# A graph network of four layers on one core: second layer's output and gate by nodes, scores straight from h, one accumulation for coordinates, taps with high passes first, and a new timetable of steps

## The chip, the cores and the metric

One NeuronCore of one Trainium2 chip. The metric is device time in microseconds (us) for one execution, which handles 16 graphs of 512 nodes with 128 features. TensorE is called PE, VectorE DVE, ScalarE ACT, GpSimd POOL, and SyncE, which only issues transfers here, SP.

## The reference

Each layer l does `h = relu(layernorm(x)); x = x + L_l(h, adj)`, for graphs of 512 nodes. Cut to what matters:

```python
# layer 0: attention with 8 heads over the adjacency, sigmoid at the end
# layer 1
h' = h @ W_w.T + W_b
e = (h' @ A) @ h'.T;  e = e + e.T
att = softmax(where(adj > 0, e, NEG), axis=1) * adj
hp = relu(att @ h')
c = sigmoid(h . gate_w[:128] + hp . gate_w[128:] + gate_b)     # one number per node
out = c * h + (1 - c) * hp
# layer 2: 5 times a message over adj and a GRU cell
# layer 3
xc = relu(bn2(conv17(relu(bn1(conv1(h))))) + h)
s = h @ w_se.T + b_se                                          # 3 coordinates
dist = |s_n|^2 + |s_m|^2 - 2 s_n . s_m;  nmp = (exp(-dist) * adj) @ relu(h @ w_msg.T + b_msg)
out = gru([xc, nmp], h)
```

## The kernel before, in words

**Slots.** Graph g uses the buffers and the four banks of accumulator memory (`banks`, B) of slot g % 2, so at most two graphs are in flight. A graph goes through `values`, `keys`, `heads`, `layer1`, `layer2`, `layer3` and `taps` on PE and through functions of the same kind on the other engines.

**Order.** Each engine has a set of generators per graph. The code between two `yield`s is one step. `in_order` (L145) merges all steps of all graphs into one fixed queue per engine, by the due times in `TURN` (L86) plus `g * GAP` (L83). The due times set the order of the queue and nothing else: every step still waits on semaphores. A step that waits holds back all that is queued behind it on its engine. There are 180 PE steps for a graph.

**Precision.** A weight or an activation is split into a high and a low part (fp32r), and a product takes three matmuls, `mm3` (L440): `high` (L445) issues high x high and low x high, `low` (L450) issues the third. Other products are plain f32. In the trace an f32 matmul shows as two MATMUL records, a transpose or an fp32r matmul as one.

**Layer 0, heads.** Each head has four tiles: DVE adds the mask and takes a minimum (L1087), ACT does a Prelu and an Exp (L802, L808), DVE a reciprocal (L1099), POOL multiplies (L395), PE transposes (L551), DVE and ACT copy (L1109, L820), PE multiplies (L557).

**Layer 1** (PE L574 to L634, ACT L822 to L851, DVE L1111 to L1197, POOL L398 to L414). h is transposed to features by nodes; h' (`h1`, L593) comes from it, then t1 = (A + A^T) h' (L598), then four score tiles (L583 to L587), each masked with a maximum on DVE (L1120), negated (L1126) and exponentiated on ACT (L838). After the fourth, DVE takes reciprocals (L1169) and scales all four tiles of h' (L1173), DVE and POOL multiply by the adjacency (L1132, L411), and PE sums hp over four tiles as features by nodes, 128x512 each (L623). The gate is two f32 matmuls with gate_w broadcast to all 128 columns (L617, L628), a 128x512 tanh (L845), two DVE operations (L1183, L1186), four transposes back (`transpose_out`, L632), an add to the residual X (L1043), then statistics, rstd on POOL (L365), normalising (L1017) and transposes for layer 2 (L634, L484). POOL also rebuilds h as one f32 tile (`whole`, L367), for L617, L1179 and, in layer 3, for L704, L713 and L1281.

**Layer 3.** Coordinates come from h by an f32 matmul (L704), their squares (L903) by two more with a matrix of -1, and twice the coordinates by another (L713 to L716), into two banks, each split by ACT and DVE (L910, L914, L1275). The convolution of 17 taps is 17 times mm3 (`taps`, L755). After it come `c2_scaled` (L1281), two Relus on ACT (L926, L927), and the matmuls of the gates (L740 to L750).

## Time and profile before

| | |
|---|---|
| median of 3 runs | 2485.11 us (2477.29 to 2489.0) |
| the profiled execution's own time | 2485.19 us |
| its span, first to last instruction | 2483.4 us |
| busy: PE, DVE, ACT, POOL | 88%, 66%, 62%, 32% |
| granted TensorE clock, mean | 0.945 of full |
| transfers (DMA) | 65.44 MB, mean 26 GB/s |
| chain that ended last | PE 60%, DVE 20%, ACT 9%, issue 8%, POOL 3% |

A busy PE is not PE at its peak: matmuls are pipelined and their records overlap, so what one costs is read from start to start. The granted clock has two levels here, full (2.4 GHz) and half (1.2 GHz). The chain that ended last is followed back from the last instruction, at each step to what released it.

### The profile page before, as it was taken

How to read it: one execution, taken by the hardware profiler on the slowest of the kernel's cores; microseconds unless marked ns; L12 is line 12 of the kernel's file. 1: busy time of each engine (PE TensorE's matmuls, PEld its weight loads, DVE VectorE, ACT ScalarE, POOL GpSimd, SP SyncE). 2: the span in 40 equal slices, each digit the busy share in tenths (PEclk: the TensorE clock that was granted, in tenths of full speed). 3: DMA queues.
4: the chain of work that ended last, by engine and by line, in shares of the span. 5: the costliest groups of instructions: out<-in, count | busy, mean ns of one | idle time of the engine just before them, and what ended most of it. 6: DMA issues, size and time to landing. Idle time of an engine off the chain costs nothing.

```text
span 2483.4 us, 35526 instructions
## 1 busy us (share of the span) xinstructions
PE 2191.5 (88%) x12414; PEld 1800.1 (72%) x12414; DVE 1635.4 (66%) x4499; ACT 1551.5 (62%) x2980; POOL 782.5 (32%) x865
## 2 busy tenths in 40 slices
PE   4779999899999989999899989989998998999866
PEld 3658777686877868777686867768687776868644
DVE  3557676675767767576775758677576767767542
ACT  1738476583856748485684848668484765848432
POOL 0323324233332423334232333424233342423311
PEclk7979999999999999999999999999999999999988
DMA  3010101010010100000010010101001010100100
GB/s 109 18 39 1 34 26 35 26 31 14 17 35 26 35 26 18 22 22 35 26 35 26 1 35 27 35 26 35 26 1 35 26 35 26 35 9 1 35 5 5
DMA packets 46788, 65.44 MB, mean 26 GB/s; under 512 B 3728, under 2 KB 21392, under 8 KB 46352
## 3 DMA queue, kind: packets, MB, share of 16 engines
q1 hardware_dynamic: 46608, 63.16, 7.8%
q8 instruction: 98, 1.61, 0.3%
q14 instruction: 82, 0.67, 0.1%
HBM read 58.96 MB, written 4.19 MB: 25 GB/s over the span
## 4 chain that ended last, share of the span: by engine, by line
PE 60%; DVE 20%; ACT 9%; issue 8%; POOL 3%; DMA 0%; DVEq 0%; SPq 0%; ACTq 0%
PE banks L557 12%; PE banks L447 8%; PE banks L448 8%; PE banks L451 8%; PE banks L551 6%; PE banks L660 3%; PE banks L664 2%; PE banks L736 2%; DVE F L1217 2%; POOL rstd L365 2%; PE banks L623 2%; ACT F L856 2%; DVE F L1224 2%; PE banks L647 2%; DVE F L1204 1%
## 5 line engine op out<-in xcount | busy, mean ns | idle before, releaser
L557 PE MATMUL banks<-F,PT 128*128 128x128 f32 x4096 | 568.4, 283 | 37.6 <-DVE PT L1109 34.5
L557 PEld LDWEIGHTS banks<-F,PT 128*128 128x128 f32 x4096 | 527.8, 198 | 68.1 <-DVE PT L1109 47.0
L856 ACT ACTIVATE F<-banks,dcols 128x512 f32<-128x512 f32 x288 | 196.2, 681 | 162.7 <-PE banks L451 161.2
L395 POOL TENSOR_SCALAR U<-U,rden 128x512 f32<-128x512 f32 x192 | 151.4, 791 | 330.7 <-DVE rden L1099 330.7
L1109 DVE COPY PT<-banks 128x512 f32<-128x512 f32 x256 | 175.3, 685 | 62.2 <-PE banks L551 61.2
L395 POOL TENSOR_SCALAR tiles<-tiles,rden 128x512 f32<-128x512 f32 x192 | 132.8, 694 | 183.4 <-DVE rden L1099 183.3
L820 ACT ACTIVATE PT<-banks 128x512 f32<-128x512 f32 x256 | 150.9, 589 | 53.5 <-PE banks L551 51.9
L551 PE MATMUL banks<-ident,U 128*128 128x128 f32 x768 | 126.3, 295 | 65.0 <-POOL U L395 65.0
L1099 DVE RECIPROCAL rden<-den 128x1 f32<-128x1 f32 x512 | 80.2, 158 | 131.6 <-ACT tiles L808 64.5
L447 PE MATMUL banks<-R,WH 128*128 128x512 f32 x352 | 157.1, 446 | 3.7 <-DVE R L1289 2.9
L1204 DVE SCALAR_TENSOR_TENSOR F<-F 128x512 f32<-128x512 f32 x96 | 71.0, 739 | 133.0 <-ACT F L856 133.0
L551 PEld LDWEIGHTS banks<-ident,U 128*128 128x128 f32 x768 | 100.6, 154 | 75.3 <-POOL U L395 69.1
L802 ACT ACTIVATE tiles<-tiles,QN 128x513 f32<-128x513 f32 x192 | 137.2, 715 | 20.5 <-DVE tiles L1087 20.5
L395 POOL TENSOR_SCALAR adjT<-adjT,rden 128x512 f32<-128x512 f32 x128 | 88.9, 694 | 192.4 <-DVE rden L1099 192.4
L447 PE MATMUL banks<-HS,WH 128*128 128x512 f32 x336 | 147.7, 440 | 1.4 <-ACT HS L783 1.4
L808 ACT ACTIVATE tiles<-tiles 128x512 f32<-128x512 f32 x192 | 138.7, 722 | 13.4
L451 PE MATMUL banks<-R,WH 128*128 128x512 f32 x352 | 145.6, 414 | 0.0
L808 ACT ACTIVATE U<-U 128x512 f32<-128x512 f32 x192 | 138.2, 720 | 9.6
L421 POOL TENSOR_TENSOR HS<-HT,HS 128x512 fp32r<-128x512 f32 x64 | 83.0, 1297 | 193.9 <-ACT HS L885 193.9
L802 ACT ACTIVATE U<-U,QN 128x513 f32<-128x513 f32 x192 | 137.4, 716 | 9.1 <-DVE U L1087 9.0
L448 PE MATMUL banks<-R,WLO 128*128 128x512 f32 x352 | 141.6, 402 | 0.0
L448 PE MATMUL banks<-HS,WLO 128*128 128x512 f32 x336 | 140.2, 417 | 0.0
(217 smaller groups left out, 5574.2 us busy)
## 6 DMA issues: line engine op xcount, KB each, us to landing
adjN<-in_adj_dram SPq DMA_DIRECT2D x32, 1024.0 KB, 5.2
adjT<-in_adjt_dram SPq DMA_DIRECT2D x16, 1024.0 KB, 5.2
xin<-in_x_dram SPq DMA_DIRECT2D x18, 256.0 KB, 2.8
out_dram<-X SPq DMA_DIRECT2D x16, 256.0 KB, 2.3
F<-in_c2w_dram SPq DMA_DIRECT2D x1, 1088.0 KB, 7.7
F<-in_wraw_dram SPq DMA_DIRECT2D x1, 1024.0 KB, 9.4
PT<-in_fcw_dram SPq DMA_DIRECT2D x1, 512.0 KB, 3.8
PT<-in_fpw_dram SPq DMA_DIRECT2D x1, 512.0 KB, 4.6
```

What stands on the lines that cost most here:

```text
L395: pool.tensor_scalar(SC[s][h % RING][:, t, 0:NODES], SC[s][h % RING][:, t, 0:NODES], rden[s][:, t:t + 1], 1.0, ALU.mult, ALU.mult).then_in ...
L447: pe.matmul(dst, w[0], xs[0], start=start, stop=False)
L448: pe.matmul(dst, w[1], xs[0], start=False, stop=False)
L451: return pe.matmul(dst, w[0], xs[1], start=False, stop=stop)
L551: last = pe.transpose(pt_bank(s, j)[:, part(t)], SC[s][h % RING][:, t, part(j)], ident[:, :])
L557: last = pe.matmul(B[s][:, 3, part(j)], PT[s][:, k, part(j)], G[s][:, k, h * DIM:(h + 1) * DIM], start=(h == 0 and j == 0 and k == 0), sto ...
L802: act.activation(SC[s][h % RING][:, t, :], SC[s][h % RING][:, t, :], ACT.Prelu, bias=QN[s][:, t, h:h + 1], scale=0.01, alpha=100.0).then_i ...
L808: act.activation(SC[s][h % RING][:, t, 0:NODES], SC[s][h % RING][:, t, 0:NODES], ACT.Exp, bias=SC[s][h % RING][:, t, NODES:NODES + 1], sca ...
L820: act.activation(PT[s][:, j, :], pt_bank(s, j), ACT.Copy).then_inc(S["pt_act"], 1)
L856: act.activation(F[s][:, tile, :], B[s][:, bank, :], func, bias=dcol(bias), scale=0.5)\
L1109: dve.tensor_copy(PT[s][:, j, :], pt_bank(s, j)).then_inc(S["pt_dve"], 1)
L1204: dve.scalar_tensor_tensor(F[s][:, 3, :], F[s][:, 0, :], 1.0, F[s][:, 2, :], ALU.add, ALU.mult)\
```

## The change

What it does, by parts:

1. **Scores straight from h.** W_w^T (A + A^T) is multiplied out once in the setup (`WA`), so that t1 (negated) comes from h in the same PE step as h', and not from h'. The signs are turned: DVE adds +9e15 and takes a minimum, ACT uses it as a bias with scale -1, and the negation (L1126) is gone.
2. **Output by nodes.** Reciprocals and scaling go tile by tile. hp is summed with the attention as the stationary operand: 4 x 4 f32 matmuls of 128 columns in place of 4 of 512.
3. **Gate by nodes.** The two gate matmuls, the 128x512 tanh and the four transposes back go. In their place: 2 x 4 dot products with accumulation on DVE (128x128), a 128x4 tanh on ACT, two 128x512 adds on POOL, and four 128x128 operations on DVE that write X.
4. **Coordinates in one accumulation.** mm3 with `se` and one f32 matmul of 4 rows in place of four f32 matmuls. POOL's `whole` is no longer waited for there; in layer 1 it is gone.
5. **Taps.** 17 steps of `high` (two matmuls) that wait only for the high part of the first convolution, then 17 steps of `low`. POOL adds the batch norm's shift to h ahead of time (`x_shift`), and one Relu on ACT goes. The matmuls of nmp come ahead of those of xc.
6. **`transpose_in`** waits for each of the four normalised tiles by itself.
7. **A new `TURN`** for all engines, GAP 139.637 for 140.9, 195 PE steps for a graph.

The core of the diff:

```diff
@@ PE, layer1
-                    pe.matmul(B[s][:, t % 2, :], R[s][:, 2, part(t)], R[s][:, 1, :], start=False, stop=False)
                     if t == 0:
                         pe.wait_ge(*after("t1_low", g))
-                    pe.matmul(B[s][:, t % 2, :], R[s][:, 3, part(t)], R[s][:, 0, :], start=False, stop=True) ...
+                    pe.matmul(B[s][:, t % 2, :], R[s][:, 3, part(t)], R[s][:, 0, :], start=False, stop=False)
+                    if t == 0:
+                        pe.wait_ge(*after("h1_low", g))
+                    pe.matmul(B[s][:, t % 2, :], R[s][:, 2, part(t)], R[s][:, 1, :], start=False, stop=True)\
...
+                high(B[s][:, 2, :], W("WA"), (HH[s], HL[s]))
                 high(B[s][:, 1, :], W("Ww"), (HH[s], HL[s]))
...
-                pe.matmul(B[s][:, 0, :], col("gw1").broadcast_to([P, P]), HT[s][:, :], start=True, stop=False)
                 for t in range(TILES):
                     yield
+                    pe.wait_ge(*after("h1_scaled", g, t + 1))
                     pe.wait_ge(*attended(g, t))
-                    last = pe.matmul(B[s][:, 2, :], F[s][:, 1, part(t)], PT[s][:, t, :], start=(t == 0), ...
+                    for i in range(TILES):
+                        last = pe.matmul(B[s][:, 2, part(i)], PT[s][:, t, part(i)], F[s][:, 1, part(t)], ...
-                pe.matmul(B[s][:, 0, :], col("gw2").broadcast_to([P, P]), F[s][:, 2, :], start=False, stop=True)\
-                transpose_out(g, Y[s])
@@ PE, layer3
-                pe.matmul(B[s][0:AUG, 2, :], cols[:, CI["se0"]:CI["se0"] + AUG], HT[s][:, :])\
+                mm3(B[s][0:AUG, 2, :], W("se", 0, AUG), (HH[s], HL[s])).then_inc(S["s3_banked"], 1)
...
-                pe.matmul(B[s][0:AUG, 0, :], se2[:, :], HT[s][:, :], start=True, stop=False)
-                pe.matmul(B[s][0:AUG, 2, :], neg5[:, 1, :], F[s][0:AUG, 2, :], start=False, stop=True,
-                pe.matmul(B[s][0:AUG, 0, :], neg5[:, 0, :], F[s][0:AUG, 2, :], start=False, stop=True)\
+                pe.matmul(B[s][0:AUG, 2, :], cols[0:ROWS5 - 1, CI["nq0"]:CI["nq0"] + AUG], F[s][0:ROWS5 - 1, 2, :],
@@ DVE, layer1
-                def negative_max(t):
+                def scaled_rows(t):
+                    dve.wait_ge(*after("s_exped", g, t + 1))
+                    dve.reciprocal(rden[s][:, t:t + 1], den[s][:, t:t + 1]).then_inc(S["rden1"], 1)
...
+                def gate_dots(of, side, a, signal):
+                    for t in range(TILES):
+                        last = dve.tensor_tensor_reduce(out=F[s][:, 3, part(t)], in0=F[s][:, of, part(t)],
...
-                dve.scalar_tensor_tensor(F[s][:, 5, :], F[s][:, 3, :], 1.0, F[s][:, 4, :], ALU.add, ALU.mult)\
-                dve.scalar_tensor_tensor(Y[s], F[s][:, 5, :], 0.5, F[s][:, 2, :], ALU.mult, ALU.add)\
-                add_residual(g, 1)
+                dve.wait_ge(*after("x_h_hp", g))
+                for t in range(TILES):
+                    last = dve.scalar_tensor_tensor(X[s][:, t, :], F[s][:, 4, part(t)], gate[s][:, 0, t:t + 1],
+                                                    F[s][:, 7, part(t)], ALU.mult, ALU.add)
@@ POOL, layer1
-                whole(g, 0)
+                pool.tensor_tensor(F[s][:, 6, :], X[s][:, :, :]..., F[s][:, 5, :], ALU.add)
...
+                pool.wait_ge(*after("x_h", g))
+                pool.wait_ge(*after("hp", g))
+                pool.tensor_tensor(F[s][:, 7, :], F[s][:, 6, :], F[s][:, 2, :], ALU.add).then_inc(S["x_h_hp"], 1)
```

What the new `TURN` makes of three places of the queues (older graph: layers 2 and 3; next graph: the one a slot behind it):

- **PE, layer 1 of the next graph.** Before: h', three taps of the older graph, t1, three taps, scores with a tap among them, three more taps, the gate matmul L617, hp of tiles 0 and 1, gates of layer 3 (21 matmuls), hp of tiles 2 and 3, L628, transposes back. After: h' and t1, nmp tiles 2 and 3, the last tap, all scores, gates of layer 3 (21 matmuls), hp tiles 0 and 1, `transpose_in` of the graph after, hp tiles 2 and 3, then of that graph `values` steps 1 and 2 (the qk matmuls and the first mm3), the transposes out of the older graph, `values` step 3, the first keys, `values` steps 4 and 5, and the transposes into layer 2.
- **DVE, the same place.** After: four masked tiles with the scaled tiles and both adjacency products among them, then the whole GRU cell of layer 3 of the older graph, `h_low` of the graph after, the hp dot products, the older graph's last residual, X.
- **POOL, rstd of layer 3.** Before it stands between the second and the third normalised tile of head 6 (due 136.0, 137.0 after 132.5). After it stands before the first tile of head 6, and PE has head 5's last steps, the first matmuls of layer 3 and four taps between it and head 6's first transposes. ACT's queue holds the first six ACT steps of layer 3 from the last softmax step of head 6 to those of head 7; before, the first stood ahead of the very last softmax step and the others behind it. All of layer 2's ACT steps lie between softmax steps in both.

## Rows read from the trace of the kernel before

**Rows 1.** One line's first and last instruction: the gate matmul L617, once per graph

```profile
L617 PE MATMUL banks<-HT,cols x32: 591/592/667, 161.5 to 2347.6; 128*128 128x512 f32 x32
L617 PE MATMUL banks<-HT,cols x16: 591/592/593, 448.6 to 1476.1; 128*128 128x512 f32 x16
```

**Rows 2.** Busy time by stretch: stretch, length, PE, PEld, DVE, ACT, POOL, clock, DMA share, GB/s

```profile
1184.95:1332.39 147.44, 135.46 (x772) 111.64 (x772) 101.22 (x280) 96.13 (x186) 49.14 (x53) 0.95 0.08 26
1205.00:1295.00 90.00, 80.90 (x524) 71.41 (x523) 69.25 (x202) 74.53 (x148) 32.45 (x39) 0.96 0.11 36
1223.00:1283.00 60.00, 59.39 (x415) 53.37 (x414) 45.50 (x120) 52.85 (x105) 21.23 (x26) 1.00 0.01 1
1283.00:1300.00 17.00, 12.96 (x84) 11.42 (x84) 13.96 (x52) 12.07 (x25) 10.75 (x11) 0.90 0.37 124
1331.00:1361.00 30.00, 24.78 (x99) 17.33 (x100) 19.70 (x53) 14.09 (x26) 3.93 (x5) 0.89 0.17 53
```

**Rows 3.** Waits of PE from 1184 to 1328 us: us, times, longest

```profile
PE banks L551 <- POOL U L395: 4.0, 1, 4.0
PE banks L484 <- DVE hN L1017: 2.0, 1, 2.0
PE banks L623 <- DVE F L1173: 2.0, 1, 2.0
PE banks L557 <- DVE PT L1109: 1.9, 2, 1.8
PE banks L647 <- ACT HT L849: 0.7, 1, 0.7
```

**Rows 4.** Timeline of PE: start, length, line, operation

```profile
1299.18 1.02 PE L713 MATMUL banks<-HT,se 128*101 128x512 f32 x2
1300.04 1.02 PE L714 MATMUL banks<-F,neg 101*101 101x512 f32 x2
...
1301.76 0.60 PE L551 MATMUL banks<-ident,tiles 128*128 128x128 f32 x4
1302.19 1.06 PE L557 MATMUL banks<-F,PT 128*128 128x128 f32 x8
1303.09 0.60 PE L551 MATMUL banks<-ident,tiles 128*128 128x128 f32 x4
...
1308.52 0.40 PE L448 MATMUL banks<-C,WLO 128*128 128x512 f32 x1
1308.76 0.40 PE L451 MATMUL banks<-C,WH 128*128 128x512 f32 x1
```

**Rows 5.** Timeline of POOL around its rstd of layer 3

```profile
1285.26 1.03 POOL L365 TENSOR_TENSOR rstd<-var,mhalf 128x4 f32<-128x4 f32 x1 [3.06 <-DVE var L1011]
1286.28 1.36 POOL L395 TENSOR_SCALAR U<-U,rden 128x512 f32<-128x512 f32 x2
```

**Rows 6.** Timeline of PE behind its wait in layer 1

```profile
1187.97 0.63 PE L448 MATMUL banks<-R,WLO 128*128 128x512 f32 x1
1188.39 0.63 PE L451 MATMUL banks<-R,WH 128*128 128x512 f32 x1
```

**Rows 7.** Timelines of POOL and DVE in layer 1 of the last graph

```profile
2345.73 1.29 POOL L411 TENSOR_TENSOR PT<-U,adjT 128x512 f32<-128x512 f32 x1 [0.48 <-ACT U L838]
...
2345.32 0.68 DVE L1120 CUSTOM_DVE_ANT_0 U<-U,banks 128x512 f32<-128x512 f32 x1 [0.52 <-issue]
...
2345.93 1.64 DVE L1132 TENSOR_TENSOR PT<-U,adjT 128x512 f32<-128x512 f32 x1
...
2349.01 1.13 DVE L1173 TENSOR_SCALAR F<-banks,rden 128x128 f32<-128x128 f32 x4
2350.05 0.68 DVE L1132 TENSOR_TENSOR PT<-U,adjT 128x512 f32<-128x512 f32 x1
```

**Rows 8.** The chain that ended last, from a residual's add to the transposes into layer 2

```profile
1349.34 0.61 DVE X L1043
...
1354.52 0.67 PE banks L484 x4
```

More of the change, by code:

```diff
@@ L75 @@
+    "msg_banked": 1, "msg": 1, "dist_banked": 4, "dist_exped": 4, "weights3": 4, "c2_banked": 1, "c2_scaled": 1, "x_shift": 1, "xc_high": 1,
     "xc_low": 1, "nmp_banked": 1, "nmp_high": 1, "nmp_low": 1,
 }
-OWN = {"stats": 4, "aggregated": 4, "variance": 4, "rstd": 4, "normed": 4, "h_banked": 4, "h_high": 4, "h_low": 4,
-       "h": 3, "y_banked": 3, "residual": 4}
-GAP = 140.9
+OWN = {"stats": 4, "aggregated": 4, "variance": 4, "rstd": 4, "normed": 16, "h_banked": 4, "h_high": 4, "h_low": 4,
+       "h": 2, "y_banked": 2, "residual": 4}
@@ L133 @@
-    ("DVE", "tile_copies"): (73.0, 76.4, 85.1, 89.6, 96.4, 101.6, 108.7, 113.0, 117.1, 123.2, 128.8, 132.4, 140.1,
[8 rows of a table removed]
+    ("SP", "transfers"): (0.00, 54.05, 100.46, 160.66, 228.53, 273.98),
+    ("Pool", "inputs"): (108.65, 114.18, 215.01),
+    ("Pool", "normalized"): (133.59, 138.29, 146.24, 146.76, 147.77, 147.98, 154.53, 154.79, 162.59, 164.84, 164.84,
[24 rows of a table added]
+    ("Activation", "values"): (129.60, 131.75, 137.34, 148.99, 157.74),
+    ("Activation", "softmax"): (140.05, 140.05, 141.33, 143.14, 148.10, 153.31, 153.31, 154.50, 155.07, 155.07,
[5 rows of a table added]
@@ L352, in _ @@
             pool.wait_ge(setup_pool, 1)
-            for b in range(BLOCKS):
-                pool.memset(neg5[0:3, 0, 32 * b + 3:32 * b + 4], -1.0)
-                last = pool.memset(neg5[0:3, 1, 32 * b + 4:32 * b + 5], -1.0)
-            last.then_inc(setup_pool, 1)
             pool.wait_ge(setup_dve, 1)
@@ L412, in layer1 @@
                         .then_inc(S["att_pool"], 1)
+                yield
+                pool.wait_ge(*own("residual", g, 0))
+                pool.wait_ge(*after("h_half", g))
+                pool.tensor_tensor(F[s][:, 6, :], X[s][:, :, :].rearrange("p t n -> p (t n)"), F[s][:, 5, :], ALU.add)\
+                    .then_inc(S["x_h"], 1)
+                yield
+                pool.wait_ge(*after("x_h", g))
+                pool.wait_ge(*after("hp", g))
+                pool.tensor_tensor(F[s][:, 7, :], F[s][:, 6, :], F[s][:, 2, :], ALU.add).then_inc(S["x_h_hp"], 1)
                 yield
@@ L427, in layer3 @@
                 yield
-                whole(g, 2)
+                whole(g, 3)
+                yield
+                pool.wait_ge(*own("h", g, 1))
+                pool.tensor_scalar(F[s][:, 4, :], HT[s][:, :], dcol("sh2"), 1.0, ALU.add, ALU.mult)\
+                    .then_inc(S["x_shift"], 1)
                 for t in range(TILES):
@@ L760, in taps @@
                         pe.wait_ge(*after("msgt", g))
+                        pe.wait_ge(*after("c1_high", g, 1))
+                    high(B[s][:, 3, :], W("c2", k), (C1[s][:, 0, k:k + NODES], C1[s][:, 1, k:k + NODES]), start=(k == 0))
+                for k in range(TAPS):
+                    yield
+                    if k == 0:
                         pe.wait_ge(*after("c1_low", g))
-                    last = mm3(B[s][:, 3, :], W("c2", k), (C1[s][:, 0, k:k + NODES], C1[s][:, 1, k:k + NODES]),
-                               start=(k == 0), stop=(k == TAPS - 1))
+                    last = low(B[s][:, 3, :], W("c2", k), (C1[s][:, 0, k:k + NODES], C1[s][:, 1, k:k + NODES]),
+                               stop=(k == TAPS - 1))
                 last.then_inc(S["c2_banked"], 1)
@@ L1319 @@
     fpw = wide(v["L0_gnn_fp_w"].reshape(HEADS, DIM, DIM).transpose(1, 0, 2))
+    se = _np.zeros((P, 104), _np.float32)
+    for b in range(BLOCKS):
+        se[:, 32 * b:32 * b + 3] = v["L3_gnn_w_se"].T
     wraw = _np.concatenate([
@@ L1341, in blocks, with rows @@
         return z
-    one, none = _np.ones(ROWS5, _np.float32), _np.zeros(ROWS5, _np.float32)
-    b_se, e3, e4 = v["L3_gnn_b_se"], _np.eye(ROWS5, dtype=_np.float32)[3], _np.eye(ROWS5, dtype=_np.float32)[4]
+    def rows(*values):
+        return _np.array(values, _np.float32)
+    none = rows(0, 0, 0, 0, 0)
+    moving, still = rows(1, 1, 1, 0, 1), rows(2, 2, 2, 1, 0)
+    moving_one, still_one = rows(0, 0, 0, -1, 0), rows(0, 0, 0, 0, -1)
+    nq = _np.zeros((P, AUG), _np.float32)
+    for b in range(BLOCKS):
+        nq[0:3, 32 * b + 3:32 * b + 5] = -1.0
+        nq[3, 32 * b:32 * b + 3] = v["L3_gnn_b_se"]
     columns = _np.concatenate([
```

279 lines of the change are left out of this document (132 added, 147 removed), and 86 rows, old and new, of the table TURN.

## The prediction

> **What bounds the kernel now.** First, one line's first and last instruction give the period: L617 runs once per graph, 16 graphs lie 2186 us apart, and seven graphs in the middle take 1027.2 us between the first's start and the eighth's, 146.7 us each [rows 1]. So a microsecond per graph is 15 us in the end; the other 285 us are the first graph's way in and the last one's way out. Second, busy time by stretch: over one period PE is busy 135.5 of 147.4 us with a mean granted clock of 0.95, ACT 96.1, DVE 101.2, POOL 49.1 [rows 2]. PE is the bound, but not everywhere: in the middle of the heads it is busy 59.4 of 60 us beside an ACT at 52.9 (88%), from 1283 to 1300 only 13.0 of 17, in layer 1 24.8 of 30 [rows 2]. Third, the waits: five waits make 10.6 us a period, and the largest, 4.0 us, is a transpose waiting for POOL [rows 3]. Fourth, the clock: behind a 2.0 us wait an fp32r matmul takes 0.42 us from start to start [rows 6], where it takes 0.24 at full clock [rows 4]: that is the 1.2 GHz level against 2.4. At a mean of 0.95 a period loses some 7 us to it. A period is thus about 129 us of work at full clock, 11 of stalls and 7 of half clock.
>
> **Work on PE.** From start to start an f32 matmul of 512 columns costs 0.86 us, four f32 matmuls of 128 columns 0.90, four transposes 0.43, an fp32r matmul 0.24 [rows 4]. Removed per graph: two gate matmuls (1.72), four transposes (0.43), L704, L713, L714 and L716 (3.44), in all 5.59. Added: three fp32r matmuls for the coordinates (0.72), one f32 matmul (0.86), and hp in 4 x 4 narrow ones (4 x 0.04 = 0.16), in all 1.74. The added f32 matmul has 4 rows, which no row shows; 101 rows cost the same as 128 [rows 4], so I take 0.86, with 0.24 as the low end. WA for As, and high passes of taps ahead of low ones, are the same number of matmuls. **-3.85 us.**
>
> **The POOL stall.** Before, POOL's queue has the rstd of layer 3 between two tiles of head 6. It waits 3.06 us for the variance, then runs 1.03, and only then come the tiles for which PE stands still [rows 5]. The new queue has it ahead of head 6's first tile, and PE has transposes, products, nine matmuls of layer 3 and four taps (over 6 us) before it needs that head. The rstd still delays POOL, but what is late next is covered: four tiles at 0.7 us fit in those 6 us. I let the 4.0 us go, and with it the half clock behind it, 0.10 of 17 us [rows 2]. Bounds: 0 (the wait only moves to head 6's first tile) and 5.7. **-5.7 us.**
>
> **Start of heads.** The 1.9 us on L1109 [rows 3] come from a product that follows its own transposes. The new order puts two matmul steps of layer 2 (0.9 us) and transposes between; the copy needs some 0.7, so 0.6 stay: **-1.3 us**. But the first cell of layer 2 has fewer steps of others behind it: keys and three mm3, 2.6 us, where the cell's chain wants about 3.6 behind its last matmul; before, transposes and products filled most of that. Bounds 0 and 1.1: **+0.7 us.**
>
> **Layer 1.** Here chains get shorter, and PE's queue gets less to do beside them. I go along the new queues from the end of the first score tile. DVE, at 0.61 us for an operation on 128x512 [rows 7], from 2345.32 to 2345.93: four masked tiles 3.0, four scaled ones 1.8 (four of 128 columns take 1.13), two low parts 1.2, two adjacency products 2.3 (0.68 alone, 1.64 beside POOL's), a wait for the last Exp 0.6, layer 3's cell 3.6, h_low of the graph after 0.6: 13.1 us. PE beside it: nine score matmuls and transposes 2.6, the 21 matmuls of layer 3 5.0, hp 3.6, transposes 0.4: 11.6. Then qk needs h_low: stall 1.5. From there DVE does the dot products of hp (2 x 4 small products in all, four of them in the path, 0.28 and an accumulator read of 0.08 each by the nearest rows: 1.4 us; between 1.1 and 2.4, the price of four whole 128x512 ones), waits for the older graph's transposes (at 2.7 us), adds, writes X (four of 128 columns, 0.5 more than the one add of before) and goes on as today, where a residual's add to the transposes takes 5.2 us [rows 8]: 2.7 + 5.2 + 0.5 + 0.4 for qk - 0.7 since the transposes start with the first tile = 8.1. PE has 5.1 us to do there: stall 3.0. The ACT wait of 0.7 [rows 3] stays. In all 5.2, against 2.0 + 2.0 + 0.7 before [rows 3]: +0.5.
>
> One more price: the trace shows an adjacency product of DVE, two inputs from SBUF, taking 1.64 us while POOL's product runs, and 0.68 without it [rows 7]. The new POOL add `x_h_hp` (1.29 us, as L411) is released by hp, just as the four dot products of hp with two inputs each are. So I add 0.9, between 0 and 1.3. The Trainium skill, SBUF — State Buffer, section Who interferes with whom, says that a DVE instruction with two SBUF inputs contends with a GpSimd instruction that reads SBUF, and that whoever comes second is blocked for the whole instruction. By that rule the term would be up to 1.3 if POOL comes first, and 20 us in the run. **Layer 1: +1.4 us.**
>
> DVE and ACT in total: DVE gets some 2.4 us more, ACT 1.2 less (the 128x512 tanh and one Relu), POOL about 2 more of 49; off the path, except as said.
>
> **Everything else in the new timetable.** 195 PE steps have new neighbours. I followed layer 1, the rstd and the start of heads; where I looked at layer 2's later cells, 3.9 to 5.2 us of heads stand behind each cell's last matmul, which is enough. What I have not followed can hold new stalls: none, or as many as there are now (10.6). I take 4, the size of today's largest. The due times themselves I use as an order and not as a time.
>
> **Sum.** -3.85 - 5.7 - 1.3 + 0.7 + 1.4 = -8.75; with 4, -4.75 us per graph: a period of 142.0. Times 15 is -71. Once per run: the way out of the last graph loses the t1 hop, the gate matmul and the transposes back, `whole`, two accumulations and a Relu, some 7 to 8 us; setup gains two matmuls, two DVE operations and a wider copy, 1 to 2. Together -6. The profiled execution took 2485.2 (span 2483.4), which is the median of the runs shown (2485.1) as near as one can say: 2485.2 - 71 - 6 = **2408 us**.
>
> **A second way to the period.** In the stretch of the heads (1205 to 1295) ACT is busy 74.5 us [rows 2]. The new queue adds the first six ACT steps of layer 3 to it (5.7), 80.2 busy. At the 88% of the middle of the heads that is a stretch of 91.1, at the 83% of the whole one (74.5 of 90) 96.6. The rest of the period is PE's: 37.4 us of matmuls (24 tap steps, layer 3 from the distances on, layer 1, values), 6.1 of stalls, 3.3 of half clock (0.11 of 30 us [rows 2]): 46.8. The period is then 137.9 or 143.4; my 142.0 lies between.
>
> **Rivals.**
> *A, all goes as followed.* No new stalls: -8.75 x 15 - 6 = 2348 us. For it: each price has a row. Against it: every queue is new, and each engine waits in order.
> *B, the saved work stood in waits.* L617 stands right ahead of the 2.0 us wait on L1173, L628 and the transposes near the end of the chain, so 2.15 of the 3.85 come back as stall; with unseen stalls of 6.6 all is eaten: -8.75 + 2.15 + 6.6 = 0, 2479 us, no change. For it: DVE is the engine that ends all waits of layer 1 but one [rows 3]. That the change leaves the machine's path as it was is in this case too.
> *C, slower: ACT binds in the heads.* With layer 3's first steps among the softmax steps, ACT holds up attention tiles and PE both, and its share in the stretch falls below the 83% of now. At 78% the stretch is 102.8 and the period 149.6: +2.9 x 15 - 6, 2523 us. It decides at 79%, where the stretch reaches 101.1 and the run is 0.5% slower. For it: PE and ACT now both have some 90% work in that stretch. Against it: 88% was held for 60 us at full clock [rows 2], and the worst part of the 90 us was the rstd's stall.
>
> **How the numbers follow.** My forecast 0.52; A, anything below some 2380, 0.20; B 0.16, C 0.12. About 0.5%, 12 us, can be told from no change. Faster by more: the forecast, A and half of B, 0.80; same 0.08; slower, C, 0.12. The range runs from A (2348) to 2480, B's end; above it lies C and little else.
>
> **What would show it.** L617's successor, the 128x4 tanh, should come every 142 us. The L551 wait of 4.0 us should be gone from the waits, with the clock at 1.00 there. Before the qk matmuls a wait of 1 to 2 us, before the transposes into layer 2 one of about 3, on DVE. hp at 0.90 per tile. ACT's share from the first to the last softmax step 83% or more. I am wrong if the period is above 146, if a wait over 3 us stands in the heads, or if dot products take more than 0.6 us each.

## The result: 2304.6 us, and the profile after

Median 2304.64 us in 4 runs (2300.43 to 2312.14), against 2481.2 for the kernel before in the same session: ratio 0.929, 95% interval 0.925 to 0.933. That is 7.1% faster, where 2408 us was forecast with 2348 as the low end. The sign was right, the size less than half: 77 us expected, 177 measured. The profiled execution took 2306.8 us (span 2304.9).

First the period, and what lies around it. The first product of a head, the first hp matmul of graph 0 and that of the last graph cut a span in four. First and last start of these lines, kernel before:

```profile
L557 PE MATMUL banks<-F,PT x256: 274/275/582, 71.3 to 142.8; 128*128 128x128 f32 x128
L623 PE MATMUL banks<-PT,F x8: 593/593/697, 164.3 to 167.4; 128*128 128x512 f32 x8
L623 PE MATMUL banks<-PT,F x8: 592/592/697, 2350.2 to 2358.2; 128*128 128x512 f32 x8
```

and the kernel after (graph 0, graph 0, the last):

```profile
L570 PE MATMUL banks<-F,PT x256: 275/275/582, 67.9 to 120.8; 128*128 128x128 f32 x128
L635 PE MATMUL banks<-F,PT x32: 273/275/348, 138.8 to 144.0; 128*128 128x128 f32 x32
L635 PE MATMUL banks<-F,PT x32: 273/275/275, 2184.9 to 2188.4; 128*128 128x128 f32 x32
```

| us | before | after | difference |
|---|---|---|---|
| until the first hp | 164.3 | 138.8 | -25.5 |
| from there to the last graph's hp, 15 periods | 2185.9 (145.7 each) | 2046.1 (136.4 each) | -139.8 |
| from there to the end | 133.2 | 120.0 | -13.2 |

So 140 of the 178 us of span are in the period, -9.3 us per graph, and 39 us come once per run. The start holds some noise: the first product of a head came between 67.3 and 74.1 us in the seventeen profiled executions, so differences of the first row under some 6 us say nothing. Here it came 3.4 us earlier than before; counted from it, the first hp comes after 70.9 us for 93.0, 22.1 less.

Second, PE's waits of 463 to 1463 us, some 7.3 periods of the kernel after; they are set beside [rows 3]:

```profile
PE banks L497 <- DVE hN L1020: 17.9, 17, 1.1
PE banks L458 <- DVE HS L1026: 11.9, 7, 1.7
PE banks L652 <- DVE HT L1240: 10.5, 7, 1.5
PE banks L458 <- DVE X L1045: 5.5, 7, 0.8
PE banks L458 <- DVE F L1066: 1.9, 7, 0.3
PE banks L570 <- DVE PT L1111: 0.3, 1, 0.3
```

No wait is for POOL any more, and none is longer than 1.7 us. They make 48.0 us, or 6.9 for each of seven graphs. All waits of the kernel before make 82.8 us in the same thousand, 11.8 a graph; the 10.6 of [rows 3] leave out three small ones (0.6, 0.4, 0.2).

Third, busy time by stretch: from 1250 to 1330 in the heads, and 15 us of layer 1, to set beside [rows 2]:

```profile
1250.00:1330.00 80.00, 78.53 (x516) 68.24 (x515) 63.66 (x188) 73.86 (x148) 30.41 (x39) 1.00 0.13 44
1235.00:1250.00 15.00, 12.78 (x47) 9.58 (x47) 10.51 (x39) 3.16 (x7) 3.26 (x2) 0.66 0.06 17
```

In the heads PE is busy 98% and ACT 92%, at full clock: ACT didn't become the bound, it reached a higher share than the 88% of before. In the period from 1205 to 1341.4 us half clock is now in one place, layer 1, where the mean of 15 us is 0.66 and the stretches on both sides show 1.00.

### The profile page after: what moved, and what is told of

Its sections match the earlier page's. It is cut to its first block, busy times and chain, and to the rows that moved or that the text cites. A ratio compares the mean times of both kernels' runs of the same rounds, so it can differ in the third digit from the quotient of the medians.

```text
span 2304.9 us, 36323 instructions
## 1 busy us (share of the span) xinstructions
PE 2104.6 (91%) x12626; PEld 1769.8 (77%) x12626; DVE 1671.8 (73%) x4784; ACT 1508.9 (65%) x2964; POOL 792.6 (34%) x888
## 3 DMA queue, kind: packets, MB, share of 16 engines
q8 instruction: 100, 1.64, 0.3%
## 4 chain that ended last, share of the span: by engine, by line
PE 68%; DVE 17%; ACT 4%; issue 3%; POOL 2%; DVEq 0%
PE banks L570 19%; PE banks L564 9%; PE banks L458 9%; PE banks L459 8%; PE banks L462 7%; DVE hN L1020 4%; PE banks L665 3%; PE banks L669 3%; PE banks L736 3%; POOL rstd L365 2%; PE banks L652 2%; ACT F L866 2%; PE banks L545 2%; DVE bst L1006 1%; DVE PT L1138 1%
## 5 line engine op out<-in xcount | busy, mean ns | idle before, releaser
L570 PE MATMUL banks<-F,PT 128*128 128x128 f32 x4096 | 544.8, 276 | 4.6 <-DVE PT L1111 3.5
L570 PEld LDWEIGHTS banks<-F,PT 128*128 128x128 f32 x4096 | 506.5, 192 | 18.8 <-DVE PT L1111 7.8
L395 POOL TENSOR_SCALAR U<-U,rden 128x512 f32<-128x512 f32 x192 | 138.7, 733 | 347.3 <-DVE rden L1101 347.3
L866 ACT ACTIVATE F<-banks,dcols 128x512 f32<-128x512 f32 x288 | 191.6, 682 | 14.1 <-PE banks L462 11.4
L458 PE MATMUL banks<-HS,WH 128*128 128x512 f32 (+1 forms) x368 | 170.9, 464 | 1.5 <-ACT HS L794 1.4
L365 POOL TENSOR_TENSOR rstd<-var,mhalf 128x4 f32<-128x4 f32 x64 | 79.7, 1245 | 258.9 <-DVE var L1014 258.9
L428 POOL TENSOR_TENSOR HS<-HT,HS 128x512 fp32r<-128x512 f32 x64 | 82.8, 1294 | 242.2 <-ACT HS L895 242.2
L459 PE MATMUL banks<-HS,WLO 128*128 128x512 f32 (+1 forms) x368 | 148.2, 403 | 0.0
L1020 DVE TENSOR_SCALAR hN<-X,mv,rstd 128x128 f32<-128x128 f32 x192 | 115.0, 660 | 40.1 <-POOL rstd L365 40.1
L458 PE MATMUL banks<-R,WH 128*128 128x512 f32 x336 | 135.1, 402 | 1.4 <-DVE R L1300 1.4
L462 PE MATMUL banks<-R,WH 128*128 128x512 f32 x336 | 133.1, 404 | 0.0
L462 PE MATMUL banks<-HS,WH 128*128 128x512 f32 (+1 forms) x368 | 129.9, 402 | 0.0
L497 PE MATMUL banks<-ident,hN 128*128 128x128 f32 x256 | 56.2, 312 | 79.0 <-DVE hN L1020 77.8
L1089 DVE CUSTOM_DVE_ANT_0 U<-adjN,banks 128x512 f32<-128x512 f32 x192 | 127.5, 678 | 0.0
```

The source lines that it names most:

```text
L395: pool.tensor_scalar(SC[s][h % RING][:, t, 0:NODES], SC[s][h % RING][:, t, 0:NODES], rden[s][:, t:t + 1], 1.0, ALU.mult, ALU.mult).then_in ...
L458: pe.matmul(dst, w[0], xs[0], start=start, stop=False)
L459: pe.matmul(dst, w[1], xs[0], start=False, stop=False)
L462: return pe.matmul(dst, w[0], xs[1], start=False, stop=stop)
L570: last = pe.matmul(B[s][:, 3, part(j)], PT[s][:, k, part(j)], G[s][:, k, h * DIM:(h + 1) * DIM], start=(h == 0 and j == 0 and k == 0), sto ...
L866: act.activation(F[s][:, tile, :], B[s][:, bank, :], func, bias=dcol(bias), scale=0.5)\
```

## The experiments

All edits but two (e4 and e11, which add unused matmuls) are edits of due times, so they change the order of queues and no work. Where a `TURN` is mapped, each step got the due time of the step that does the same work in the other kernel.

**e1: the new arithmetic in the old order.**

```diff
-GAP = 139.637
-TURN = {...new...}
+GAP = 140.9
+TURN = {...old, steps mapped one to one...}
```

> New arithmetic in the old order: the old due times for every strand, the steps of layer 1, layer 3 and the taps mapped one to one, GAP 140.9. Theory O (most of the gain is the order): only the 3.85 us of PE work per graph and a few us of chain are left, so about 2400 to 2420 us, with the 4.0 us POOL wait in the heads still there and the first score matmul of graph 0 near 155 us. Theory W (the arithmetic and its shorter chains gave most of it): 2330 to 2350 us and the waits of layer 1 nearly gone.

Measured 2440.1 us (2434.9 to 2441.0), ratio 0.983 [0.979, 0.987]. That is above both branches of the expectation. By the ratios, the arithmetic alone gives 43 us of the 177. First and last start, and the waits of 463 to 1463 us:

```profile
L568 PE MATMUL banks<-F,PT x256: 274/275/582, 73.3 to 142.0; 128*128 128x128 f32 x128
L633 PE MATMUL banks<-F,PT x32: 273/275/348, 158.5 to 163.7; 128*128 128x128 f32 x32
L633 PE MATMUL banks<-F,PT x32: 272/275/275, 2306.4 to 2314.7; 128*128 128x128 f32 x32
```
```profile
PE banks L562 <- POOL U L393: 28.3, 7, 4.0
PE banks L502 <- DVE accY L1238: 21.3, 7, 3.1
PE banks L568 <- DVE PT L1109: 13.7, 15, 1.8
```
```profile
1170.34 1.64 DVE L1238 SCALAR_TENSOR_TENSOR accY<-F 128x512 f32<-128x512 f32 x1
```

The period is (2306.4 - 158.5) / 15 = 143.2, 2.5 below before. The 4.0 us on POOL are untouched, and a new wait of 3.1 us stands where the older graph's transposes want the last state of layer 3's cell. DVE is done with it at 1171.98, PE with what stands ahead of the transposes some 3 us before. One of the three is contention: the last operation of the cell takes 1.64 us for 0.69, beside the new POOL add `x_h_hp`, which runs from 1169.95 to 1171.42. All waits of the thousand make 81.9 us, as many as the 82.8 before.

**e2: the old arithmetic in the new order**, the other half: `TURN` and GAP of the kernel after, mapped to the steps of before.

> Old arithmetic in the new order, the steps mapped back (one tap step is three matmuls again, the gate matmuls and the transposes back put among the values steps). Theory O: about 2481 minus two thirds of 176, some 2365 us, the POOL wait gone, the first layer 1 of graph 0 as early as in the changed kernel (near 133 us). Theory W: about 2440 us. If both orders cost the same with either arithmetic, e1 and e2 add up to the whole 176 us; if they need each other, they add up to less.

Measured 2539.2 us (2535.8 to 2543.6), ratio 1.023 [1.019, 1.028]: by the ratio 58 us slower than before, which neither theory had.

```profile
PE banks L487 <- DVE hN L1020: 43.5, 14, 4.1
PE banks L450 <- DVE X L1046: 19.7, 7, 2.9
```

The POOL wait is gone here too, but PE now waits for hN at the transposes into layer 1 and again at those into layer 2, some 3 us each (4.1 at most), and for X between them. Layer 1's chain, with its gate matmuls, wide tanh, transposes back and negation, is longer than the work that the new order leaves beside it; that reading of the waits wasn't tested by itself. So the parts don't add up: -43 for the one, +58 for the other, -177 together. Both theories priced them as a sum; the expectation named the other case, but with no number.

**e3: POOL's rstd of layer 3 behind the first tile of head 6** (kernel after).

```diff
-    ("Pool", "layer3"): (361.81, 373.24, ...
+    ("Pool", "layer3"): (368.60, 373.24, ...
```

> The changed kernel with one step of POOL's queue moved back: rstd of layer 3 behind the first normalised tile of head 6 rather than ahead of it (the old place was behind the second). As forecast, the place of this step was worth 5.7 us per graph: 2385 to 2395 us, with a wait of 4 us in the heads or before the transposes into layer 3. Rival: the wait of before was not made by the place alone, but by attention tiles made too late for PE; then 2305 to 2320 us.

2303.2 us (2296.5 to 2304.5): no difference, as the rival had it or a little better. The new order doesn't depend on the place that my step named.

**e4: eight unused matmuls in the 1.7 us wait** (kernel after, values step 1). They write to a part of the bank that is free there, and add no work to the result.

```diff
+                if g >= SLOTS:
+                    for _ in range(8):
+                        pe.matmul(B[s][:, 3, 128:512], WH[:, 0:DIM], WH[:, 0:384])
                 pe.wait_ge(*own("h_low", g, 0))
```

> The changed kernel with eight extra matmuls of 384 columns (about 1.4 us, their result is not used) ahead of the wait of the qk matmuls, where PE stands still for 1.7 us per graph and then runs at half clock for some 11 us. Theory K (the half clock there costs time): it stays at full clock and each graph gets 3 to 5 us shorter, 2235 to 2260 us. Theory D (the chain on DVE sets the pace of this stretch): the clock stays up, but the time comes back as a wait of about 3 us before the transposes into layer 2, 2295 to 2310 us.

2299.7 us (2296.8 to 2305.7), 5 us at most, in theory D's range. The mean clock rose from 0.953 to 0.964, the wait on HS fell from 11.9 to 1.5 us, and the wait on hN rose:

```profile
PE banks L497 <- DVE hN L1023: 22.4, 20, 2.0
```

In layer 1, where the next matmul waits for DVE in any case, a faster PE arrives earlier and waits. Half clock is nearly free there; e11 below shows it again.

**e5 and e6: only the rstd moved, in the old order** (e1): behind the fourth tile of head 6, and ahead of the first.

```diff
-    ("Pool", "layer3"): (276.90, 284.90, ...
+    ("Pool", "layer3"): (278.65, 284.90, ...     # e5
+    ("Pool", "layer3"): (271.10, 284.90, ...     # e6
```

> Edit: the old order with the new arithmetic (e1, 2440 us), and in POOL's queue the rstd of layer 3 goes behind the fourth tile of head 6 instead of between its second and third. Theory P (the place of the rstd in POOL's queue makes the 4.0 us wait on POOL U, as the prediction has it): the wait is gone or under 1 us, and with it 4.0 us and some 1.7 of half clock per graph: 15 x 4.0 to 5.7, so 2355 to 2380 us. Theory T (the wait is there because layer 2 as a whole ends too late in the old order; POOL only shows it): the wait moves to the transposes of layer 3 or to another tile, and the time stays at 2425 to 2440 us.

> Edit: the same kernel (e1, 2440 us) with the rstd ahead of the first tile of head 6, the place that the new timetable gives it. Theory P as the prediction's step on the POOL stall says it (early placement frees the tiles): the wait goes, 2355 to 2380 us. Theory T: the variance is not there before 1260 us of the profiled run of e1, whatever the queue, so both first tiles now wait as well and the wait on POOL grows to 5 to 8 us: 2455 to 2500 us. If T holds, what counts in the new timetable is when layer 2 ends against head 6, not the place of the rstd.

Measured 2459.5 (2453.2 to 2467.8) and 2460.0 us (2456.8 to 2464.5), both about 20 us slower than e1. e6 came as its theory T had it; e5 is slower than both of its branches. The wait on POOL U, in e5 and in e6:

```profile
PE banks L562 <- POOL U L393: 21.7, 7, 3.1
```
```profile
PE banks L562 <- POOL U L393: 37.6, 7, 5.4
```

The place that the new timetable gives to the rstd makes the wait longer in the old order. And with the rstd behind the tiles the wait falls only to 3.1; e5's DVE and POOL say why:

```profile
1261.80 1.11 DVE L1040 SCALAR_TENSOR_TENSOR X<-banks,nm,X 128x128 f32<-128x128 f32 x4
1262.95 0.87 DVE L1004 BATCH_NORM_STATS2 bst<-X 128x6 f32<-128x128 f32 x4
...
1264.35 0.26 DVE L1099 RECIPROCAL rden<-den 128x1 f32<-128x1 f32 x2
...
1264.61 1.36 POOL L393 TENSOR_SCALAR U<-U,rden 128x512 f32<-128x512 f32 x2 [3.14 <-DVE rden L1099]
```

The tiles wait for their reciprocals, which on DVE are queued behind the residual and the statistics of the same layer 2: 2.6 us, from 1261.80 to 1264.35. Two queues hold the same chain ahead of the same tiles.

**e9: both out of the way.** e5 and, on DVE, the two reciprocals ahead of the residual: `("DVE", "layer3")` starts at 277.00 for 274.50.

> Edit: the old order with the new arithmetic (e1, 2440 us); DVE's two reciprocals of the third and fourth tile of head 6 go ahead of layer 2's last residual and statistics, and POOL's rstd of layer 3 behind the fourth tile of head 6. Theory Q (the wait on POOL U is made by two queues: the rstd on POOL and, ahead of it on DVE, 2.6 us of adds and statistics): both are out of the tiles' way, so the wait falls from 4.0 us to under 1. Where the time goes is then open between two: if heads and layer 3 have slack, 2375 to 2400 us; if layer 3 is the late one (theory T), its start is another 2 to 4 us later, PE waits there for hN or for products instead, and the time stays at 2430 to 2460 us.

2480.8 us (2478.9 to 2485.7), 41 us slower than e1, and slower than either branch of the expectation. The wait on POOL U went to 2.2 us and not under 1, and PE now waits for the chain that gave way, at layer 3's first transposes, among others:

```profile
PE banks L568 <- DVE PT L1109: 26.6, 28, 1.8
...
PE banks L495 <- DVE hN L1018: 15.7, 14, 2.0
PE banks L562 <- POOL U L393: 15.3, 7, 2.2
```

Three placements of one step, all slower than the old one. The queues of POOL and DVE do set how long that one wait is (5.4, 3.1 or 2.2 us for 4.0), but the time isn't won by them: what leaves this wait comes back in others. That points to the chain from the end of layer 2 to layer 3, which comes when PE has too little beside it; e12 and e13 ask that.

**e12: take that cover away from the kernel after.** In its PE queue nine steps (eight of heads and one of keys) stand between the transposes out of layer 2 and layer 3's first transposes; the old order has six. e12 puts the former behind the nine, and DVE's residual one copy later.

```diff
-    ("PE", "layer3"): (348.04, 350.30, ...
+    ("PE", "layer3"): (349.72, 350.30, ...
-    ("DVE", "layer3"): (351.82, 352.20, ...
+    ("DVE", "layer3"): (352.40, 352.50, ...
```

> Edit: the changed kernel (2304 us); on PE the transposes out of layer 2 go behind four steps of heads instead of ahead of them (6.2 us of cover taken away from the chain residual, statistics, rstd, normalise), and DVE's residual one copy later. Theory T (in the new timetable these head steps between the end of layer 2 and layer 3's first transposes are what hides POOL's rstd; their cover is what the old order lacked): PE waits 4 to 6 us per graph for hN at layer 3's first transposes, with half clock behind: 15 x 4.5 to 7.5, 2370 to 2420 us. Rival (other slack takes it): under 2330 us.

2408.5 us (2401.0 to 2414.7): 104 us slower than the kernel after, as theory T had it. One row of the timeline of PE, and the waits:

```profile
1239.22 1.24 PE L497 MATMUL banks<-ident,hN 128*128 128x128 f32 x4 [4.61 <-DVE hN L1020]
```
```profile
PE banks L497 <- DVE hN L1020: 49.9, 24, 4.6
PE banks L458 <- DVE HS L1026: 12.0, 7, 1.7
```

(The queue moves past nine steps, and not past four as the expectation says.) The wait is 4.6 us where there was none, and the period goes from 136.4 to 143.2: 6.8 us for one step of PE, with one of DVE a copy later. It is a wait for hN, though, and not the wait on POOL U of the old order. The wait on HS and those below it stay as they were.

**e13 and e14: give the old order the cover.** In e1 every step of layers 0 and 1 becomes due up to 6 us later (ramp from 100 to 130 us, back to 0 at 200), in e14 up to 12 (ramp from 70 to 125).

```diff
+    def later(t):    # e13; applied to the due times of layers 0 and 1, all engines
+        return t + 6 * min(max((t - 100) / 30, 0), 1, max((200 - t) / 40, 0))
```

> Edit: the old order with the new arithmetic (e1, 2440 us), with one thing changed on all engines: every step of layers 0 and 1 of a graph that falls due between 100 and 200 us is due up to 6 us later (a ramp from 100 to 130, 6 until 160, back to 0 at 200). Against the older graph's layer 2 the heads are then later: 39 head steps ahead of the transposes out of layer 2 instead of 46, nine between them and layer 3's first transposes instead of five. Theory T (what the new timetable gave to the heads is this cover, whatever else it moves): the wait of 4.0 us on POOL U goes, with its half clock, and the run gains 15 x 2.5 to 5.5: 2357 to 2402 us. Rival (the rest of the new order is needed as well; a waits moves to layer 2's cell or to layer 1): 2425 us or more.

> Edit: as e13, but 12 us later at most, on a ramp from 70 to 125 and back to 0 from 165 to 200 us: 35 head steps ahead of the transposes out of layer 2, nine between them and layer 3's first transposes, 21 steps from the former to head 6 (as in the new timetable; 13 in e13, 4 in the old one). Theory T: the wait on POOL U is gone too, but the last cell of layer 2 has only three head steps of cover and layer 1 is squeezed against layer 3, so not better than e13: 2360 to 2410 us. Rival: the more the heads are late the better, below e13 by 10 us or more.

2485.5 (2482.1 to 2492.7) and 2915.5 us (2903.8 to 2923.4). e13 came as its rival had it, e14 outside both branches. Theory T as I put it, cover alone, failed. The waits of e13:

```profile
PE banks L568 <- DVE PT L1109: 19.8, 20, 1.8
PE banks L502 <- DVE HT L1238: 14.1, 7, 2.0
PE banks L502 <- DVE accY L1238: 12.6, 6, 2.1
PE banks L710 <- ACT F L908: 12.1, 7, 2.2
PE banks L456 <- ACT HS L792: 8.8, 7, 1.3
PE banks L456 <- DVE R L1298: 8.1, 6, 1.4
```

The wait on POOL is gone, as expected, but all waits of the stretch make 99 us, where e1 has 82. The transposes out of layer 2 now wait 2.0 us for HT, since fewer head steps stand ahead of them; the waits at L710, on ACT's HS and on R are new as well, 2.2, 1.3 and 1.4 us, and PT grew from 13.7 to 19.8. Cover that is moved uncovers what it stood beside. Since all engines' queues were shifted, e13 doesn't show whether the wait on POOL went by PE's cover or by the new places on POOL and DVE. In e14 (mean clock 0.90) the largest group is the first matmuls of layer 2's cells with 59.3 us, up to 4.0 a time.

**e15: the taps among the last heads** (kernel after). 14 steps of high passes go from between the steps of heads 6 and 7 to behind them.

```diff
-    ("PE", "taps"): (363.08, 365.13, 365.13, 366.18, 369.95, ..., 392.14, 393.21, 394.19, ...
+    ("PE", "taps"): (393.70, 393.70, 393.70, 393.70, 393.70, ..., 393.70, 393.70, 394.19, ...
```

> Edit: the changed kernel (2304 us) with one thing moved on PE: the 14 steps of high passes of taps (28 matmuls, 6.5 us) that stand between the steps of heads 6 and 7 go behind the last of them, next to the other 20. Nothing else moves. Theory S (the taps split into high and low passes are cover, as the head steps are: PE has them for the stretch in which ACT is the busy engine, and taken away there they leave PE waiting for tiles and copies in heads 6 and 7): new waits of 3 to 6 us per graph there, 2350 to 2400 us. Rival (the stretch from 1245 to 1340 us had slack on ACT, or the filler moves into layer 1 and shortens its waits by as much): within 10 us of 2304.

2319.1 us (2315.0 to 2323.7): 14 us slower, between the two. New waits of 1.5, 1.2 and 0.7 us come in the heads, and the largest of layer 1 falls from 17.9 to 2.5:

```profile
PE banks L570 <- ACT PT L831: 10.6, 7, 1.5
PE banks L564 <- POOL U L395: 8.2, 7, 1.2
...
PE banks L570 <- DVE PT L1111: 5.4, 8, 0.7
PE banks L497 <- DVE hN L1020: 2.5, 5, 1.0
```

So the taps as cover of the heads are worth something, but a small part of the 134 us that the timetable brings with the new arithmetic.

**e7: the first graph's layer 0 in the new order**, the rest of e1 as it was.

```diff
-            running.append((steps, [g * GAP + at for at in TURN[engine, strand.__name__]]))
+            running.append((steps, [g * GAP + at for at in of(g)[engine, strand.__name__]]))
```

> Edit: e1 (old order, new arithmetic), but graph 0 alone takes the steps of its layer 0 (values, keys, heads, softmax, denominators, tile copies, normalised tiles) in the new order. Theory F (some 16 of the 25 us that are gained once per run come from the order of the first graph's heads, where nothing of an older graph stands between): heads of graph 0 take 53 to 56 us instead of 68.7, and the run 2422 to 2428 us. Rival (the first graph's way in is set by later steps, or the gain is eaten by the second graph): 2435 to 2442 us.

2428.7 us (2426.9 to 2430.7), 11.4 below e1, a little short of the forecast. The heads of graph 0:

```profile
L602 PE MATMUL banks<-F,PT x256: 275/275/582, 67.5 to 128.5; 128*128 128x128 f32 x128
```

They take 61.0 us from the first product to the last, 68.7 in e1 and 52.9 in the kernel after: half of what the order does there. No older graph stands beside them, so part of their pace is the order of their own steps. The other half needs more than layer 0's steps of this graph; which of them wasn't tried.

**e8: POOL's scaling of adjN out of layer 1** (kernel after). In the timeline of the kernel after, DVE's four normalised tiles take 4.8 us at one place, where they take 1.1 elsewhere; here are DVE, POOL and PE there:

```profile
1211.91 4.77 DVE L1020 TENSOR_SCALAR hN<-X,mv,rstd 128x128 f32<-128x128 f32 x4 [1.12 <-POOL rstd L365]
...
1211.84 1.29 POOL L443 TENSOR_TENSOR PT<-U,adjT 128x512 f32<-128x512 f32 x1
...
1213.36 1.90 POOL L380 TENSOR_SCALAR adjN<-adjN 128x2048 f32<-128x2048 f32 x1
1215.33 2.50 POOL L443 TENSOR_TENSOR PT<-U,adjT 128x512 f32<-128x512 f32 x2
...
1215.39 0.33 PE L497 MATMUL banks<-ident,hN 128*128 128x128 f32 x1 [1.10 <-DVE hN L1020]
1216.74 0.33 PE L497 MATMUL banks<-ident,hN 128*128 128x128 f32 x1 [1.02 <-DVE hN L1020]
```

POOL works almost without a pause from 1211.84 to 1217.83, beside DVE's 1211.91 to 1216.68. One by one, the four tiles start at 1211.9, 1213.1, 1213.4 and 1215.2 and take 1.30, 0.34, 1.94 and 1.43 us: each slow one starts next to a POOL operation (1.29, 1.90 and 1.25 us) and ends about when that does.

```diff
-    ("Pool", "inputs"): (108.65, 114.18, 215.01),
+    ("Pool", "inputs"): (108.65, 124.70, 215.01),
```

> Edit: the changed kernel with one POOL step moved: the scaling of adjN for the next graph (1.9 us, 128x2048) no longer stands between layer 3's products but behind them. Theory C (contention: DVE's four normalised tiles of layer 1 take 4.8 us instead of 1.1 while POOL works, and PE's transposes wait for them 2.1 us): the wait L497 on hN falls from 17.9 to under 8 us in 463 to 1463 us, and the run gains 15 x 0.7 to 2, 2275 to 2295 us. Rival (POOL's products stand there too and block DVE just as long): the wait stays above 14 us and the time within 2298 to 2308 us.

2281.8 us (2280.0 to 2287.8), ratio to before 0.921 [0.918, 0.924]: 23 us faster than the kernel after, by one due time. Its rows:

```profile
PE banks L497 <- DVE hN L1020: 10.1, 17, 0.9
```
```profile
1198.18 4.02 DVE L1020 TENSOR_SCALAR hN<-X,mv,rstd 128x128 f32<-128x128 f32 x4 [1.12 <-POOL rstd L365]
```

The time is in theory C's range; the wait fell by 7.8 us in some seven graphs, 1.1 each, and not to under 8: POOL's three products remain beside the tiles, which still take 4.0 us. The period is (2158.5 - 138.0) / 15 = 134.7.

**e10 and e11, on top of e8.** e10 takes the low part of h ahead of the last two steps of layer 3's cell on DVE, and its high part ahead of the tanh on ACT; e11 is e8 with e4's eight matmuls.

```diff
-    ("DVE", "values"): (93.84, 98.89, 111.27, ...
+    ("DVE", "values"): (93.84, 98.89, 110.81, ...
-    ("Activation", "values"): (129.60, ...
+    ("Activation", "values"): (127.33, ...
-    ("Activation", "layer3"): (..., 406.31)
+    ("Activation", "layer3"): (..., 407.00)
```

> Edit: e8 (2282 us) and, in layer 1, the low part of h for the graph after goes ahead of the last two steps of layer 3's cell on DVE, and its high part ahead of the cell's tanh on ACT. Theory D (the 1.7 us wait before the qk matmuls is DVE's queue alone, and the older graph's transposes and X follow it): the HS wait goes from 11.9 to under 2 us in 463 to 1463 us, the clock in layer 1 rises, and the run gains 15 x 1 to 2.5: 2245 to 2267 us. Rival (what is saved there is waited for at the older graph's transposes or before layer 2): L652 and L504 waits grow by as much, 2275 to 2285 us.

> Edit: e8 (2282 us) and, as in e4, 8 unused matmuls of 384 columns in the place of the 1.7 us wait. Theory: as e4 gained 5 us on the changed kernel by keeping the clock up, with waits on hN taking half of it back, so here: 2268 to 2282 us. Rival (with the POOL scaling gone the later waits no longer take it back): 2250 to 2265 us, 15 x 1.1 to 2.1 of half clock.

2281.2 (2276.6 to 2281.7) and 2279.1 us (2273.4 to 2282.8): neither differs from e8 by what can be told. In e11 the mean clock rose from 0.957 to 0.974, and the wait on hN from 10.1 to 20.3 us in the thousand. In e10 the wait on HS is gone and the next one has taken its place, with 12.5 us in the thousand where HS had 11.9:

```profile
PE banks L458 <- DVE accY L1240: 12.5, 7, 1.8
```
```profile
1225.65 1.63 DVE L1240 SCALAR_TENSOR_TENSOR accY<-F 128x512 f32<-128x512 f32 x1
```

PE's next step wants the last state of layer 3's cell, which DVE now reaches later, and there the operation takes 1.63 us for 0.69, beside POOL's `x_h_hp` (1225.10 to 1226.74). Of all kernels run, e8, e10 and e11 are the fastest, some 1.0% below the kernel after.

## Why the prediction was wrong in size

2408 was forecast for a profiled execution that took 2306.8: 101 us too much, 60 by the allowance, 33 once per run and 8 in the sum that was followed. By the steps of the prediction:

- **The allowance for what was not followed, +4 us per graph, 60 us: the step that failed.** The followed sum was -8.75 us per graph, the measured -9.3. I priced unseen neighbours of 195 steps by today's largest wait. No new wait was over 1.7 us, and the wait that I had not seen (hN beside POOL's scaling, 2.1 us in two pieces) was balanced by one that I expected and that didn't come (3.0 us before the transposes into layer 2), which is luck. Rival A, with no allowance, was the better forecast and had 0.20, but its 2348 is 41 us too high as well. The period of 142.0 was counted from the 146.7 of seven graphs; from the 145.7 of all fifteen it would have been 141.0, and 136.4 was measured.
- **Once per run, -6 us against -39: the second largest miss, 33 us.** The way out of the last graph lost 13.2 us, not 7 to 8. The way in I took as setup only, +1 to 2; but graph 0's heads took 52.9 us from first to last product where they took 71.5 (71.3 to 142.8), 18.6 less, and the order does it (e1 68.7, e7 61.0). That there was something to win could be read in the trace of before. These are graph 0's heads, before and after:

```profile
71.00:143.00 72.00, 56.01 (x402) 52.95 (x400) 35.82 (x119) 48.77 (x100) 23.19 (x31) 0.87 0.09 30
68.00:121.00 53.00, 47.09 (x396) 44.76 (x396) 30.53 (x109) 43.89 (x92) 20.71 (x31) 0.99 0.14 46
```

PE waited 15.8 us in the first and 5.8 in the second, and the mean clock of 0.87 is worth 9 us more (0.13 of 72), that of 0.99 under 1.

- **PE's work, -3.85 us.** Where the rows allow a reading it holds: two tiles of hp took 1.79 us (1215.65 to 1217.44 in e8), 0.90 each. All of e1, work and chains, gives 2.5 us per period, since the waits stayed at 82 us in the thousand (the new one of 3.1 us for the two of 2.0 on L1173 and on hN) and the mean clock fell from 0.945 to 0.937: rival B's mechanism, in the old order.
- **The POOL stall, -5.7 us: right in size, wrong in cause.** The wait is gone and its stretch is at clock 1.00. But the place of the rstd does nothing in the new order (e3), and in the old one each other place costs time (e5, e6, e9). What the runs do show is the worth of PE's work beside the chain from layer 2's last cell to layer 3's first transposes: without it 6.8 us a graph are lost (e12), though in a wait for hN; with more of it the wait on POOL goes, and others come (e13). I had counted the cover on one side only, between the rstd and head 6, and not between the transposes out and layer 3. That this cover alone took the 4.0 us away isn't shown.
- **Start of heads, -1.3 + 0.7.** The wait on PT is gone but for 0.3 us in seven graphs, -1.9 for the -1.3 forecast. Layer 2's second cell waits 1.5 us for the state of the first (HT), where it waited for nothing before; +0.7 was forecast, with 1.1 as the bound. A wait of 0.4 ahead of the fourth cell is gone. In waits that is -0.8 against -0.6. The half clock behind the old wait on PT, 0.11 of the 15 us from 1205, was put at nothing; it is gone too, 1.6 us a graph.
- **Layer 1, stalls of 5.2 and contention 0.9.** The qk wait is 1.7 us (1.5 forecast), the four dot products 1.4 from 1235.81 to 1237.2 (1.4), and the wait of 3.0 before the transposes into layer 2 didn't come: 0.8 and 0.3 us stand there. PE had less to do in that place than DVE, but did it at half clock (0.66 in the mean of 15 us), and so was late enough. I had priced clock and wait as two costs; there they are one. The ACT wait of 0.7, which was to stay, is gone, and 2.1 us for hN stand at a place that I hadn't looked at. In all, waits on layer 1 went from 5.5 to 5.3 us and half clock from 3.3 (0.11 of 30 us) to 5.1 (0.34 of 15): +1.6 for the +1.4 forecast, near in size but by luck, as the parts differ.
- **Contention.** The price, 0.9 for an operation beside POOL's, was read from the right rows, but for the wrong neighbours: `x_h_hp` cost its partner 0.47 us (the first dot product, below, 0.75 for 0.28; in e1 and e10, beside another partner, 0.95), and POOL's scaling cost 23 us of the run (e8), in a step whose two sides the change had newly set beside each other: in the kernel before the same four tiles start at 1166.1 with no POOL operation beside them and take 0.34 us each. I had applied the rule of the Trainium skill, SBUF — State Buffer, section Who interferes with whom, to operations with two SBUF inputs alone. The same section names the tensor_scalar in its 2-port mode too, and says that whoever comes second is blocked for the whole instruction. The trace agrees: a tile of L1020, one tensor and two scalars, took 1.94 us for 0.34 beside a scaling of 1.90. In which mode it ran, no view shows.

```profile
1235.81 0.75 DVE L1144 CUSTOM_DVE_ANT_0 F<-F,cols 128x128 f32<-128x128 f32 x1
```

- **ACT in the heads.** My second way took 88% or 83% as its ceiling; it ran at 92%. Rival C didn't happen.

**What stays open.** The order and the arithmetic need each other: -43 for one, +58 for the other, -177 for both. Moving the heads as a whole (e13, e14), the rstd (e3, e5, e6, e9) or the taps (e15) in one of the two kernels never reproduces the step between them; e12 shows one place of it, worth 104 us when it is undone alone. Where the time went is seen in the waits, six kinds of at most 1.7 us, where the other orders keep one or two of 3 to 5 (e1, e2, e5, e6, e12) or, as e13, thirteen kinds of up to 2.2. Why just this order does it is not shown: a smaller set of moves that would do it was not found. Which part of the forecast -8.75 us holds can't be told to better than a microsecond or so either: with the waits and clocks read above the terms come to -10.4, and -9.3 was measured. The second half of the gain in the first graph's heads is open too.

## What to carry to other kernels

For engines that each work through a fixed queue, price a new order by cover: for each chain that leaves PE and comes back, count PE's work between the two ends, in both orders, and look at what stood beside the work that was moved. A wait that names an engine shows the last link only; before moving that link, ask when its input comes, and test with a kernel that takes the cover away. And an allowance for the unknown belongs in the range, not in the forecast, when the order was made as a whole.

## What the runs showed of the hardware

- Four DVE operations on 128x128 tiles (L1020, one tensor and two scalars per partition) took 1.1 us alone and 4.8 beside POOL's products and its 128x2048 scaling, 4.0 beside the products alone. Single ones went from 0.34 to 1.94 us, about the length of the POOL operation beside them.
- Half clock ahead of a wait on DVE cost next to nothing here: eight added matmuls raised the mean clock from 0.953 to 0.964 and gained 5 us at most, since the next wait on DVE grew from 17.9 to 22.4 us in the thousand (e4). On top of e8 they raised it from 0.957 to 0.974 for 3 us at most, and that wait from 10.1 to 20.3 (e11).
- ACT held 92% of 80 us beside a PE at 98% and full clock.
